# Four staging buffers and a 4 KB layout for the experts' first weights

## The reference

```python
# graph layer (x is the layer-normed input)
neigh = segment_sum(x[src], dst) / max(deg, 1)
h = x @ W_self + b_self + neigh @ W_neigh
x = input + prelu(layernorm(h)) + x
# experts, on xn = layernorm(x): 16 experts, top 2, D = 512, F = 256
top_vals, top_idx = top_k(xn @ gate_weight.T, 2)
routing_w = softmax(top_vals)
h = silu(einsum('td,efd->tef', xn, w1))            # w1: 16 x 256 x 512
h_mean[e] = mean of h[t, e] over the tokens t that chose e
y_mean = einsum('ef,edf->ed', h_mean, w2)
out[t] = x[t] + sum_k routing_w[t, k] * y_mean[top_idx[t, k]]
```

## Time and profile before

| | us |
|---|---|
| median of 3 runs | 1993.89 |
| lowest, highest | 1990.02, 1994.68 |
| the profiled execution's own time | 1995.32 |
| its span in the profile | 1993.6 |
| busy: PE, DVE, POOL, ACT | 1351.2, 1007.6, 939.3, 789.6 |
| transfers | 410.76 MB, mean 206 GB/s |

### The profile page before, as it was taken

How to read it: one execution, slowest core, us unless ns; L and a number is a source line. 1 busy time by engine, 2 the same in 40 slices (tenths; PEclk the granted TensorE clock), 3 DMA queues, 4 the chain that set the end, 5 groups by cost and what they waited for, 6 DMA issues and landing times.

```text
span 1993.6 us, 40990 instructions
## 1 busy us (share of the span) xinstructions
PE 1351.2 (68%) x8245; PEld 705.6 (35%) x8246; DVE 1007.6 (51%) x3228; ACT 789.6 (40%) x1745; POOL 939.3 (47%) x981
## 2 busy tenths in 40 slices
PE   1888789999565565656655655653441488999976
PEld 0444334444222222222222222222341255555512
DVE  5766425555576555655655556565553222222226
ACT  2444345555545444444444444443451133211102
POOL 1000076666777777777777777772666000000000
PEclk9999989999878878788778888886555699999985
DMA  4555388887788777777777777773664566433246
GB/s 152 178 196 196 136 279 271 277 263 262 245 264 249 224 225 226 232 229 222 225 228 234 224 224 232 228 225 94 230 220 181 175 183 183 134 93 92 84 168 257
DMA packets 174756, 410.76 MB, mean 206 GB/s; under 512 B 25968, under 2 KB 42354, under 8 KB 174648
## 3 DMA queue, kind: packets, MB, share of 16 engines
q0 software_dynamic: 75776, 244.16, 39.7%
q1 hardware_dynamic: 82636, 136.97, 20.8%
q10 hardware_dynamic: 16236, 28.57, 4.7%
HBM read 328.17 MB, written 81.43 MB: 205 GB/s over the span
## 4 chain that ended last, share of the span: by engine, by line
PE 36%; POOL 23%; issue 16%; DVE 10%; DMA 9%; ACT 4%; POOLq 2%; SPq 1%; ACTq 0%; DVEq 0%
POOL work L513 21%; PE ps L727 20%; PE ps L814 8%; DMA work<-table,work 3%; ACT work L681 2%; DMA work<-xt_d 2%; POOL bucket L530 2%; PE ps L895 2%; PE ps L938 2%; DMA wparts<-in_w_t 1%; POOLq L508 1%; DVE wparts L1313 1%; PE ps L910 1%; PE ps L957 1%; DMA bucket<-slots,work 1%
## 5 line engine op out<-in xcount | busy, mean ns | idle before, releaser
L513 POOL DMA_INDIRECT work<-table,work x832 | 818.5, 984 | 521.9 <-DMA table<-work 237.9
L814 PE MATMUL ps<-work 128*128 x2056 | 594.3, 441 | 362.8 <-DMA work<-table,work 346.8
L814 PEld LDWEIGHTS ps<-work 128*128 128x128 f16 x2056 | 219.4, 107 | 613.8 <-issue 477.7
L606 ACT ACTIVATE work<-iota_row,work 128x128 f16<-128x128 f32 x1040 | 331.8, 389 | 42.3 <-ACT work L612 31.3
L612 ACT ACTIVATE work<-work,ones 128x512 f16<-128x512 f16 x259 | 185.9, 718 | 406.7 <-PE ps L817 405.9
L727 PE MATMUL ps<-wparts,work 128*128 128x512 f16 x1176 | 283.9, 393 | 25.3 <-DVE work L1088 25.3
L1156 DVE TENSOR_SCALAR inv<-ps 128x1 f32 (+1 forms) x49 | 7.8, 158 | 383.7 <-PE ps L817 383.7
L727 PE MATMUL ps<-work,wparts 128*128 x1368 | 173.8, 275 | 27.6 <-DVE wparts L1313 15.7
L1313 DVE COPY wparts<-ps 128x1024 f16<-128x1024 f16 x114 | 78.2, 689 | 193.3 <-PE ps L895 193.3
L727 PEld LDWEIGHTS ps<-wparts,work 128*128 128x128 f16 x1176 | 117.7, 101 | 159.2 <-DVE work L1088 28.5
L727 PEld LDWEIGHTS ps<-work,wparts 128*128 128x128 f16 x1368 | 124.5, 98 | 76.6 <-issue 59.0
(11 more groups left out here) (245 smaller groups left out, 1446.4 us busy)
## 6 DMA issues: line engine op xcount, KB each, us to landing
wparts<-bucket SPq DMA_DIRECT2D x114, 256.0 KB, 2.7
work<-in_x SPq DMA_DIRECT2D x96, 256.0 KB, 3.9
work<-in_w_t SPq DMA_DIRECT2D x32, 512.0 KB, 7.2
work<-table,work POOLq DMA_INDIRECT x832
xt_d<-work SPq DMA_DIRECT2D x49, 256.0 KB, 2.6
work<-xt_d ACTq DMA_DIRECT2D x49, 256.0 KB, 4.3
table<-work SPq DMA_DIRECT2D x48, 256.0 KB, 2.1
x_d<-work SPq DMA_DIRECT2D x48, 256.0 KB
```

Source lines behind the costliest of these rows:

```text
L513: pool.indirect_dma_start(out=gath[:, g % GRING, w, :], out_offset=None, in_=table[:, :], in_offset=bass.IndirectOffsetOnAxis(ap=idx_all[: ...
L606: last = act.activation(away[:, par, w, :], iota_row[:, :], ACT.Abs, bias=negd[:, ds(GT * k + w, 1)])
L814: pe.matmul(ps[:, ds(bank, 1), :], hot[:, s, w, :], gath_row[:, ds(at + (2 * w + half) * D, D)].unsqueeze(1), start=False, stop=True, skip ...
```

## The change

`stage2` gets four buffers in place of two. SP issues the first four loads at once and loads expert `e` after the low half of expert `e - 4`. The four buffers fill `wparts` exactly (4 x 4 KB per partition). Each buffer has its own semaphore, so there are four `v_ld2` in place of two.

The host lays out the first weights anew: instead of a matrix of 512 rows by 4096 columns, from which an expert's block is read as four runs of 1 KB for each partition, each expert is 128 rows of 4 KB, one run for each partition. Both loads use it, the one into `stage` in the gather stage and the one into `stage2` in routing. The bytes are the same.

```diff
+STAGES = 4
-        stage2 = old.bitcast(f32)[:, 0:2 * CHUNKS * FF].rearrange("p (b c n) -> p b c n", b=2, c=CHUNKS)
+        stage2 = old.bitcast(f32)[:, 0:STAGES * CHUNKS * FF].rearrange("p (b c n) -> p b c n", b=STAGES, c=CHUNKS)
-        v_ld, v_ld2 = sem("v_ld"), sems("v_ld2", 2)
+        v_ld, v_ld2 = sem("v_ld"), sems("v_ld2", STAGES)
 def load_w1(it, b):
-    sp.dma_start(stage[:, :, :], w1_t[:, ds(j * FF, FF)].rearrange("(c p) n -> p c n", p=P)).then_inc(v_ld, 16)
+    sp.dma_start(stage[:, :, :].rearrange("p c n -> p (c n)"), w1_t[ds(j * P, P), :]).then_inc(v_ld, 16)
 for e in range(EXPERTS):
-    if e >= 2:
-        sp.wait_ge(v_lo, e - 1)
-    sp.dma_start(stage2[:, e % 2, :, :], w1_t[:, e * FF:(e + 1) * FF].rearrange("(c p) n -> p c n", p=P)
-                 ).then_inc(v_ld2[e % 2], 16)
+    if e >= STAGES:
+        sp.wait_ge(v_lo, e - STAGES + 1)
+    sp.dma_start(stage2[:, e % STAGES, :, :].rearrange("p c n -> p (c n)"), w1_t[e * P:(e + 1) * P, :]
+                 ).then_inc(v_ld2[e % STAGES], 16)
 def w1_high(e):
-    act.wait_ge(v_ld2[e % 2], 16 * (e // 2 + 1))
-    act.activation(w1[:, e, :, 0, :], stage2[:, e % 2, :, :], ACT.Copy, scale=wscale[:, 3:4]).then_inc(v_hi, 1)
+    act.wait_ge(v_ld2[e % STAGES], 16 * (e // STAGES + 1))
+    act.activation(w1[:, e, :, 0, :], stage2[:, e % STAGES, :, :], ACT.Copy, scale=wscale[:, 3:4]).then_inc(v_hi, 1)
 # w1_low: stage2[:, e % 2, :, :] becomes stage2[:, e % STAGES, :, :]
-        "w1_t": np.asarray(L0_ffn_w1).reshape(EXPERTS * FF, D).T,
+        "w1_t": np.asarray(L0_ffn_w1).reshape(EXPERTS, FF, CHUNKS, P).transpose(0, 3, 2, 1).reshape(EXPERTS * P, CHUNKS * FF),
```

More of the change, by code:

```diff
@@ L1210, in w1_low @@
                 dve.wait_ge(v_hi, e + 1)
-                dve.scalar_tensor_tensor(w1[:, e, :, 1, :], stage2[:, e % 2, :, :], wscale[:, 3:4], w1[:, e, :, 0, :],
+                dve.scalar_tensor_tensor(w1[:, e, :, 1, :], stage2[:, e % STAGES, :, :], wscale[:, 3:4], w1[:, e, :, 0, :],
                                          ALU.mult, ALU.subtract).then_inc(v_lo, 1)
```

## The result

The changed kernel takes 1970.75 us (median, 1968.55 to 1975.04 in 4 runs), against 1991.95 (1985.76 to 1994.68 in 4 runs) for the kernel before: a ratio of 0.990, interval 0.987 to 0.9931, or 21.2 us faster, where 19.9 were forecast (1974.0). The interval leaves room for anything from 14 to 26 us, so the runs alone don't tell one term of the forecast from another; the profile has to. The profiled execution took 1975.04 us with a span of 1973.3, 20.3 us less than the span before.

What follows compares the result with a forecast made beforehand. Routing was taken as bound by the two-buffer load loop in parts 0 to 7, then by POOL's issuing. Routing's -16.9 and the gather stage's -3.0 make -19.9 us: median 1974.0, range 1968 to 1985.

Steps and rivals of the forecast that it cites:

- The loads leave the path: Routing: ACT's waits for first-weight loads go, and with them POOL's idle time at seven part starts, 17.55 us gained.
- POOL is next, from part 0 on: Routing: once loads are early, POOL's issuing at 10.12 us per part is the bound; ACT needs 6.1 us.
- Stretched scatters: Routing: scatters issued beside DVE's low halves take longer, 7 x 0.65 = 4.5 us in place of 3.89.
- the routing term: Routing's whole gain: 17.55 + 3.89 - 4.5 = 16.9 us, between 12.6 and 19.1.
- The transfers carry it: Routing: the 16 engines have room for scatters and loads, 8.6 us of transfers per part in 10.12.
- The rival with the sign turned round: Routing: transfers are the bound, scatters land late and POOL waits, so it ends slower, 2003 us; chance 0.05.
- the one in which ACT waits and POOL with it: Routing: loads still set the pace in part, half of POOL's idle time stays, 1983 us; chance 0.08.
- The layout in the gather stage: Gather stage: loads with a quarter of the packets get out of the way of `xt_d`, 3 us gained, 0 to 6.
- The first rival: Gather stage: larger packets delay `xt_d`, 7 us lost there, 1984 us in all; chance 0.10.
- The sign named for this rival: Gather stage: PE busy less than 48 of 50 us before 510 us would show that the packets hurt.
- After the last scatter: What follows the last scatter waits for its landing and starts earlier by the same amount.

Runs made afterwards that it cites:

- The control with added ACT work: Kernel before the change, with some 1.45 us more ACT work ahead of each high half: 1997.79 us, one run; scatters' span 152.80 us in place of 145.51.
- the repeat: The changed kernel measured again with no edit, against the kernel before: 1970.81 us (6 runs), ratio 0.989.

## Why the prediction was right

*The loads leave the path* (17.55 us): exact. All seven starts of parts have 0.30 or 0.31 us in the trace, so the 17.55 us are gone in full; with the stretches, 0.5 us more were gained in routing, 18.05 in all for 16.9 forecast. The control with added ACT work shows the step from the other side.

*POOL is next, from part 0 on*: shown by the brackets, by DVE's 30.5 us of waiting for scatters, and by three edits (fewer buffers, later low halves, more on ACT) that bring ACT's waits back up to 19.9 us, or its load up by 3 us per part, and leave the span of the scatters at 127.4 to 128.1 us. One small slip in the prediction: 52.47 us over 41 intervals are 1.280 us each, with the longer scatter near the end (1.58 us) in them; 1.265 is the pace without it, and the one that the sum needs.

*Stretched scatters* (4.5 us, from 3.9): they came to 3.3 us in this profile, to 4.1 in the next and to between 3.4 and 4.5 in the others, so the size was right within 1.2 us, which is the whole error of the routing term. The prediction had named scatters of 2 us and more as a sign of being wrong; one of 2.00 us came. The limit was set too low: a scatter that meets a low half at its start must take up to 1.28 + 0.84 = 2.1 us, and that says nothing against the sum. The Trainium skill ("SBUF — State Buffer", Who interferes with whom) has the lock and whole instructions; the merged low halves agree with it (a scatter of 2.90 us beside an instruction of 2.35, where 0.96 is the ordinary length). The prediction took the rule to give 9.0 us, one whole instruction for each part; that was my reading and not the rule's, since a scatter is held for what is left of the instruction when it starts. DVE was not held in turn: its low halves take 1.279 to 1.285 us in the changed kernel's profile, also where a scatter was under way when one began (1400.28 and 1400.52). No row here bears out that part of the rule.

*The transfers carry it*: they do, at 259 GB/s. The rival with the sign turned round (a rate under 236) did not come; neither did the one in which ACT waits and POOL with it. Loads did land later (5.6 us in the median for 4.9), but with time to spare.

*The layout in the gather stage* (3.0 us): this term failed. Its step was that a load with a quarter of the packets is a shorter burst and gets out of the way of `xt_d`. The transfers of SP's queue (`q1`, in which these loads are) from 250 to 600 us, before and after: packets, MB, share of the 16 engines' time.

```profile
q1 hardware_dynamic: 11424, 14.68, 12.8%
q1 hardware_dynamic: 6048, 14.68, 12.7%
```

Half as many packets took the same time: it went by the bytes. PE's waits for `xt_d` at 250 to 510 us are 5.6, 3.0 and 1.4 us in three kernels with the old layout (the one before, the one with four buffers, the one before with more on ACT) and 3.7 to 5.2 in six with the new one and whole loads (all on chips of ordinary speed): no order in them. They vanish only with a quarter of the bytes, and there the pieces (128 of 1 KB) are as small as in the old layout and as few as in the new one. The times alone couldn't rule out 3 us: four buffers take 1971.87 us with the old layout and 1970.81 with the new one.

The first rival (the larger packets hurt) did not show either: 4 KB packets made no measurable harm. The prediction had taken it from the Trainium skill's rule on turns by packets ("DMA: Bandwidth & Descriptors", Queues, rings and completion order). But a packet of that rule holds several descriptors, while the packets counted here are single runs of 1 or 4 KB, so it is not sure that by the rule a turn grows with the run. The sign named for this rival, PE busy less than 48 of 50 us, can't tell: PE had 47.65 in one window of the kernel before already.

That the forecast came out within 1.3 us of the change measured, although this term was wrong, is partly luck. Routing gave 18.05 us. What the medians show beyond that, 3.1 us here and 2.9 in the repeat (20.3 us against 17.4 in the scatters), lies inside the intervals and has no cause shown; in the first profile it stands ahead of the first scatter (2.2 us), and the repeat's profile doesn't have it.

*After the last scatter*: nothing moved, 0.03 us, as forecast.

## What to carry to other kernels

When a transfer on the chain is issued only after its buffer is freed one step earlier, count what the next engine in line needs per step: the gain is the standing time of that engine (here POOL's 17.55 us), not the waiting time of the one that waited for the transfer (ACT's 52.2). One buffer more was enough, and the shape of the transfer was worth nothing that the runs could tell. An engine's wait that has no wait behind it, like DVE's new 30.5 us, is what a moved bound looks like, and the way to check it is to add work to the old bound and see that nothing happens.

## What the runs showed of the hardware that was not expected

DVE's low half, an instruction with two operands in SBUF, holds an indirect transfer's issue on POOL until its own end plus 0.84 us; the changeover to a second one ends the hold. Splitting a long one is worth something where POOL is the bound: a scatter that was hit lost 1.5 us in the mean with one instruction of 2.35 us, and 0.5 with two of 1.28. Whether other forms of instruction do the same was not tried.

One chip ran all kernels 20% slower, the kernel before at 2382.52 us. In routing there POOL stood for some 9.5 us at a time, three times 29.65 us apart, in the kernel with late low halves:

```profile
1823.28 1.22 POOL L531 DMA_INDIRECT bucket<-slots,work  x1 [9.35 <-DVE work L1253]
...
1852.93 0.96 POOL L531 DMA_INDIRECT bucket<-slots,work  x1 [9.49 <-DVE work L1253]
...
1882.59 0.96 POOL L531 DMA_INDIRECT bucket<-slots,work  x1 [9.55 <-DVE work L1253]
```

```profile
1816.34 1.93 ACT L659 COPY work<-ps 128x1024 f16<-128x1024 f16 x2 [9.23 <-remote]
1816.46 0.22 DVE L1223 COPY work<-ps 128x64 f32<-128x64 f32 x1 [12.28 <-remote]
```

ACT and DVE stood first, for 9.23 us (from 1807.11) and 12.28 us (from 1804.18), while POOL went on issuing scatters until 1813.94; then POOL stood for the rows that DVE made late. So the engines did not stand all at once, as an expectation above has it, and what kept ACT and DVE came first. "remote" is the profile's name for a releaser outside this core's record. What causes it stays open; no trace of the kernel before was taken there. The ratio of the kernel with late low halves holds on that chip (0.9895, 0.9899 elsewhere), the spans don't.
